# An adapter with weights made per batch: two late matmul groups moved, one batch tiled otherwise, repeated waits dropped

## The chip, the core and the metric

The kernel runs on one core of one Trainium2 chip. The metric is the device time in microseconds (us) of one execution. Three runs of the kernel before took 210.18, 210.27 and 210.38 us; the median is 210.27 us. One further execution was profiled: it took 210.3 us, and its span, from the first to the last instruction, is 208.4 us.

## The reference

Everything is float32. `x` is (4, 1024, 512): B = 4 batches, L = 1024 rows, D = 512 columns. `h` is (4, 128), one vector of H = 128 per batch, and N = 128 is the width of the bottleneck.

```
dWd  = ((h @ Wdd.T + bdd) * 0.1).reshape(B, N, D)     # Wdd is (65536, 128): 33.6 MB
dWu  = ((h @ Wdu.T + bdu) * 0.1).reshape(B, D, N)     # Wdu is (65536, 128): 33.6 MB
down = relu(einsum('bld,bnd->bln', x, Wd + dWd) + bd)
up   = einsum('bln,bdn->bld', down, Wu + dWu) + bu
out  = x + up
```

The two big matrices are each read once; `x` (8.4 MB) is read and `out` (8.4 MB) written.

## The kernel before, in words

**Two phases of loading.** Wdd and then Wdu come in 32 chunks of 1 MB each (lines 236 to 285). All loads of these, the eight 1 MB pieces of `x` and all stores are issued by SP (SyncE), in one order that is written out; an instruction that waits on SP holds everything behind it. VectorE transposes each chunk in 32x32 blocks (L315; the last chunk in two halves, L373). TensorE sums two chunks at a time against `st`, which holds the four `h` vectors (`sum_pair`, L552; `sum_last_pair`, L680), into the PSUM tiles `acc`. Four chunks make a group; ScalarE copies it (`g_rows`, L391) and TensorE turns it (`turn_down_group`, L563 and L566, in phase one; `turn_up_group`, L578, in phase two). The result is `wd_b` in phase one and `wu_b` in phase two: each group g of Wdu brings 64 of the 512 columns of `wu_b`. GpSimd adds these (L516, L519), and VectorE adds the last group (L326, L329).

**The adapter itself runs beside phase two.** The 1024 rows of a batch are 8 blocks of 128 (I = 8). Three kinds of work are interleaved on TensorE after the sums of chunk t, by the tables `TURN_AT`, `DOWN_AT` and `UP_COUNT`:

- `turn_x_unit(j)`: transposes two blocks of `x` (16 in all, j = 0 to 15), in two halves m = 2j and 2j + 1 of four transposes each (L635). ScalarE copies each half to `xt` (L433), and GpSimd adds `bu` to `x` (L500).
- `down_unit(j)`, in short D_j: the down sum of the same two blocks, four matmuls of 256 columns into the PSUM tile `dn` (L646). ScalarE copies it with ReLU to `down` (L441, `down_ready`). There is one `dn`, so D_j waits for the copy of D_(j-1).
- `up_unit(e)`, in short U_e: a number of blocks by a number of columns of the output, 512 elements per partition at most, with `down` as the stationary operand (L670). `UNITS` lists 34 of them as (batch, first block, blocks, first column, columns). A unit of four blocks by 128 columns is called quarter-D here, one of two blocks by 256 columns half-D. A unit waits for `down_ready` of all its blocks. U0 to U20 are copied by ScalarE (L451) and added to `x` in SBUF by GpSimd (L507, `pool_final`); U21 to U33 are added by VectorE straight from PSUM (L358, `dve_final`). Transposes and units share four PSUM banks in a ring (`BANK_USE`).

Every float32 matmul and transpose is recorded as two passes, so D_j has 8, a quarter-D unit 8 and a half-D unit 4 matmul records.

**The tail** begins when the last chunk has been transposed. TensorE then does, in this order: the last pair sum, X14, the last turned group, X15, U19 to U23, D14, U24, U25, D15, U26 to U33. X14 and X15 are the last two transposed pairs of blocks. D14 and D15 make the blocks 4 to 7 of batch 3, which only U30 to U33 use.

**Stores.** `STORES` has 14 of them, in SP's order after all loads: the first column halves of batches 0, 1 and 2 (1 MB each) and of half of batch 3, then the second halves in pieces of 256 or 512 KB, and last blocks 4 and 5 and blocks 6 and 7 of batch 3 over all columns (512 KB each). Each waits for the units inside it; the last one waits for U33.

Of the kernel before, what the change touches and what calls it, by code (L numbers as in the profile page):

```python
# [7 lines left out]
B, L, D, N, H = 4, 1024, 512, 128, 128  # L8
# [29 lines left out]
I = L // P  # L38
# [6 lines left out]
PIECE_OF = [j // 2 for j in range(DOWN_UNITS)]  # L45
# [7 lines left out]
HALF = D // 2  # L53
QD = D // 4
EARLY = 2
UNITS = [(b, i, 4, q * QD, QD) for q in range(2) for b in range(EARLY) for i in range(0, I, 4)]
UNITS += [(b, i, 2, 0, HALF) for b in range(EARLY, B) for i in range(0, I, 2)][:-2]
UNITS += [(b, i, 4, 2 * QD, QD) for b in range(EARLY) for i in range(0, I, 4)]
UNITS += [(2, 0, 4, 2 * QD, QD), (2, 4, 2, 2 * QD, QD), (2, 6, 2, 2 * QD, QD)]
UNITS += [(0, 0, 2, 3 * QD, QD), (0, 2, 2, 3 * QD, QD), (0, 4, 4, 3 * QD, QD)]  # L60
UNITS += [(b, i, 4, 3 * QD, QD) for b in range(1, B - 1) for i in range(0, I, 4)]
UNITS += [(B - 1, i, 2, HALF, HALF) for i in range(0, I - 4, 2)]
UNITS += [(B - 1, i, 2, c, HALF) for i in range(I - 4, I, 2) for c in (0, HALF)]
# [5 lines left out]


TURN_AT = {0: 2, 1: 3, 2: 4, 3: 5, 4: 6, 5: 7, 8: 8, 9: 9, 10: 10, 11: 11, 12: 12, 13: 13}
DOWN_AT = {0: 1, 1: 2, 2: 3, 3: 4, 4: 5, 5: 6, 6: 7, 9: 8, 10: 9, 11: 10, 12: 11, 13: 12, 15: 13}
LAST_DOWNS = (DOWN_UNITS - 2, DOWN_UNITS - 1)
assert list(TURN_AT.values()) == list(range(2, LAST_DOWNS[0]))
assert list(DOWN_AT.values()) == list(range(1, LAST_DOWNS[0]))
UP_COUNT = {8: 1, 9: 1, 14: 2, 16: 1, 17: 1, 18: 2, 19: 1, 20: 2, 21: 1, 22: 1, 23: 1, 24: 1, 25: 1, 26: 1, 27: 1, 28: 1}
UP_AT, UP_BEFORE_LAST = {}, 0
for _t, _n in UP_COUNT.items():
    UP_AT[_t] = list(range(UP_BEFORE_LAST, UP_BEFORE_LAST + _n))
# [1 line left out]


UP_BEFORE_SUM = UP_BEFORE_LAST
UP_BEFORE_DOWNS = (UP_BEFORE_SUM + 5, UP_BEFORE_SUM + 7)
assert UP_BEFORE_SUM < POOL_UNITS <= UP_BEFORE_DOWNS[0]


# [23 lines left out]
def later(count, back):  # L111

    return not isinstance(count, int) or count >= back


def hyper_adapter(nc, x, cond, Wd, bd, Wu, bu, Wdd, bdd, Wdu, bdu, out):
# [10 lines left out]
    with ctx:  # L127
# [6 lines left out]
        def sem(name):  # L134
            return ctx.enter_context(nc.semaphore(name))
# [41 lines left out]
        x_loaded = [sem(f"x_loaded{h}") for h in range(len(X_PIECES))]  # L177
# [18 lines left out]
        g_ready = sem("g_ready")  # L196
# [25 lines left out]
        def bank_of(kind, n):  # L222
            return bank[USE_OF[kind, n] % BANK_RING]
# [5 lines left out]
        def unit_size(e):  # L229
            _, rows, cols = unit_at(e)  # L230
            return (rows.stop - rows.start) * (cols.stop - cols.start)
# [149 lines left out]
        def _(act):  # L381
# [55 lines left out]
            def copy_down(j):  # L437

                act.wait_ge(down_summed, j + 1)
                b, i0 = j // BATCH_UNITS, j % BATCH_UNITS * UNIT_I  # L440
                nc.scalar.activation(down[:, b, i0:i0 + UNIT_I, :],  # L441
                                     dn[:].rearrange("p (i l) -> p i l", i=UNIT_I),
                                     ACT.Relu, bias=bd_col[:]).then_inc(down_ready, 1)
# [10 lines left out]
            def copy_x_unit(j):  # L454
                copy_x(2 * j)
                copy_x(2 * j + 1)
# [7 lines left out]
            for t in range(CHUNKS - PAIR):  # L464
# [5 lines left out]
                if t in TURN_AT:  # L470
                    copy_x_unit(TURN_AT[t])
                if t in DOWN_AT:
                    copy_down(DOWN_AT[t])
                for e in UP_AT.get(t, ()):
# [62 lines left out]
        def _(pe):  # L537
# [8 lines left out]
            def sum_pair(c, low, slot, a):  # L546

                pe.wait_ge(wt_ready, c + PAIR)
                for r in range(R):
                    for h in range(PAIR):  # L550
                        place = 2 * (r % 2) + h
                        last = nc.tensor.matmul(a[TILE * place:TILE * (place + 1)],  # L552
                                                st[:, r, low * TILE:(low + 1) * TILE], wt[:, slot + h, r],
                                                start=low == 0 and r < 2, stop=low == 1 and r >= 2)
                last.then_inc(pair_summed, 1)

            def turn_down_group(g, n):

                pe.wait_ge(g_ready, g + 1)
                if later(g, 1):  # L560
                    pe.wait_ge(group_ready, g)
                for k in range(C):
                    nc.tensor.matmul(gt[:, k, 0:PART], g_rows[:, n, k * P:(k + 1) * P], fold[:],  # L563
                                     start=True, stop=False)
                    pick = ident[:, bass.ds(g * SQ, SQ)].unsqueeze(2).to_broadcast([P, SQ, B])
                    last = nc.tensor.matmul(gt[:, k, 0:PART], base_d[:, k * P:(k + 1) * P], pick,  # L566
                                            start=False, stop=True)
                last.then_inc(g_turned, 1)
# [14 lines left out]
            def turn(it):  # L583
                for u in range(TURN_CHUNKS):
                    c, s, n = TURN_CHUNKS * it + u, u % SLOTS, u // SLOTS
                    if s == 0 and later(it, 1):
                        pe.wait_ge(g_ready, 2 * it + n - 1)
                    if s % PAIR == 0:
                        sum_pair(c, s // PAIR, u % T_RING, acc[n][:])
                    if u == 6 and isinstance(it, int):  # L590

                        pe.wait_ge(base_u_summed, 1)
                        for k in range(C):
                            last = nc.tensor.transpose(bank[1][:, k * P:(k + 1) * P], wu_nat[:, k], ident[:])  # L594
                        last.then_inc(base_turned, 1)
                        pe.wait_ge(bias_loaded, 16 * 2)
                        pe.wait_ge(ones_ready, 1)
                        nc.tensor.matmul(bank[2][:, 0:D], ones, bu_row, start=True, stop=True)  # L598
                        nc.tensor.matmul(bank[3][:, 0:1], bd_row, ones[:, 0:1], start=True, stop=True
                                         ).then_inc(bias_spread, 1)  # L600
                    if u == 1 and not isinstance(it, int):
                        turn_down_group(2 * it - 1, 1)
                    if u == SLOTS + 1:
                        if isinstance(it, int):
                            pe.wait_ge(fold_ready, 1)
                            pe.wait_ge(base_d_summed, 1)
                        turn_down_group(2 * it, 0)

            turn(0)
            with pe.Fori(1, TURNS) as it:  # L610
                turn(it)
# [17 lines left out]
            def turn_x(m):  # L629
                j, c0 = m // 2, m % 2 * BANK_C  # L630
                b, i0 = j // BATCH_UNITS, j % BATCH_UNITS * UNIT_I
                pe.wait_ge(x_loaded[PIECE_OF[j]], 16)
                wait_bank("x", m)
                for n, (c, i) in enumerate((c, i) for c in range(c0, c0 + BANK_C) for i in range(UNIT_I)):
                    last = nc.tensor.transpose(bank_of("x", m)[:, n * P:(n + 1) * P],  # L635
                                               xs[:, b, i0 + i, c * P:(c + 1) * P], ident[:])
                last.then_inc(x_turned, 1)
# [12 lines left out]
            def turn_x_unit(j):  # L650
                turn_x(2 * j)
                turn_x(2 * j + 1)
# [36 lines left out]
            down_unit(0)  # L689
            for t in range(CHUNKS - PAIR):  # L690
                c, s, g = CHUNKS + t, t % SLOTS, (CHUNKS + t) // SLOTS
                if s == 0:
                    pe.wait_ge(g_ready, g - 1)
                if s % PAIR == 0:
                    sum_pair(c, s // PAIR, t % T_RING_U, acc[g % 2][:])
                if s == SLOTS - 1:
                    turn_up_group(g)
                if t in TURN_AT:
                    turn_x_unit(TURN_AT[t])
                if t in DOWN_AT:  # L700
                    down_unit(DOWN_AT[t])
                for e in UP_AT.get(t, ()):
                    up_unit(e)
# [7 lines left out]
            turn_x_unit(LAST_DOWNS[1])  # L711
            for e in range(UP_BEFORE_SUM, UP_BEFORE_DOWNS[0]):
                up_unit(e)
            down_unit(LAST_DOWNS[0])
            for e in range(UP_BEFORE_DOWNS[0], UP_BEFORE_DOWNS[1]):
                up_unit(e)
            down_unit(LAST_DOWNS[1])
            for e in range(UP_BEFORE_DOWNS[1], UP_UNITS):
                up_unit(e)
# [26 lines left out]
```

## Time and profile before

| | |
|---|---|
| median of three runs | 210.27 us |
| the profiled execution, its span | 210.3 us, 208.4 us |
| HBM read, written | 76.55 MB, 8.39 MB |
| TensorE matmul, VectorE busy | 171.6 us (82%), 160.1 us (77%) |
| ScalarE, GpSimd busy | 57.3 us (28%), 74.1 us (36%) |
| mean granted TensorE clock | 0.946 |
| last chunk's transposes begin | 183.83 us |
| VectorE's last addition begins | 204.65 us |

Part 2 of the profile's page cuts the span into 40 slices of 5.2 us. A line of the chain of waits gives a start, a duration and what ran or was awaited. A line of the timeline gives a start, a duration, the engine (PE is TensorE's matmuls, PEld its weight loads, ACT ScalarE, POOL GpSimd, SPq a DMA issued by SyncE), the line of the kernel, the operation, the tiles, and in brackets the idle time before it and what ended that. The ends of matmuls are modelled by the profiler.

### The profile page before, as it was taken

The page shows a single profiled execution, that of the slowest core. Times are in us where ns is not written, and L with a number is a line of the kernel's source. Part 1 is how long each engine was busy: PE and PEld are TensorE (multiplying, and loading weights), DVE is VectorE, ACT ScalarE, POOL GpSimd, SP SyncE. Part 2 cuts the span into 40 slices and gives each one's busy share as a digit, 9 for nine tenths or more (in the row PEclk, how much of TensorE's full clock was granted, in tenths as well). Part 3 has the DMA queues.
Part 4 walks back from the last instruction along what each step waited for, and adds up shares of the span by engine and source line. Part 5 has one row for each costly group of instructions (what it writes and reads, how often), then busy time and mean ns, then how long its engine had stood idle before and what let it go on. Part 6 is the DMA issues. An engine that isn't in the chain of part 4 may idle for free.

```text
span 208.4 us, 3089 instructions
## 1 busy us (share of the span) xinstructions
PE 171.6 (82%) x1164; PEld 103.0 (49%) x1164; DVE 160.1 (77%) x89; ACT 57.3 (28%) x104; POOL 74.1 (36%) x59
## 2 busy tenths in 40 slices
PE   1066599847776993899999989999999988889992
PEld 0011173423321740376866748668656544549991
DVE  2868998899999999944854976468998999974373
ACT  2000014101111112043554535545425442416100
POOL 2000000000000000026857927988467977558300
PEclk9999999997975599699999999999999999999998
DMA  5999999999999999999999999999999999999998
GB/s 219 422 415 423 421 421 417 421 426 421 417 426 423 421 417 425 423 426 420 415 423 425 420 412 425 417 425 421 420 420 420 421 420 417 426 389 386 371 348 312
DMA packets 18617, 85.11 MB, mean 408 GB/s; under 512 B 1447, under 2 KB 8620, under 8 KB 9389
## 3 DMA queue, kind: packets, MB, share of 16 engines
q1 hardware_dynamic: 18592, 84.94, 99.8%
q8 instruction: 8, 0.13, 0.3%
q14 instruction: 5, 0.03, 0.0%
q10 hardware_dynamic: 12, 0.00, 0.0%
HBM read 76.55 MB, written 8.39 MB: 408 GB/s over the span
## 4 chain that ended last, share of the span: by engine, by line
DMA 64%; DVE 18%; PE 15%; issue 1%; SPq 0%; DVEq 0%
DMA w<-in_L_cond_Wdu_dram 38%; DMA w<-in_L_cond_Wdd_dram 26%; DVE wt L315 17%; PE bank L670 5%; PE acc L552 4%; PE dn L646 2%; DVE wt L373 1%; PE gt L563 1%; PE bank L635 1%; PE gt L566 1%; PE acc L680 1%; PE bank L598 1%; SPq L242 0%; DVE xs L358 0%; PE bank L594 0%
## 5 line engine op out<-in xcount | busy, mean ns | idle before, releaser
L315 DVE STREAM_TRANSPOSE wt<-w 128x2048 f32<-128x2048 f32 x63 | 145.5, 2311 | 31.9 <-DMA w<-in_L_cond_Wdu_dram 22.8
L552 PE MATMUL acc<-wt,st 128*32 128x512 f32 x496 | 72.6, 712 | 28.6 <-DVE wt L315 28.6
L500 POOL TENSOR_TENSOR xs<-xs,bu_all 128x1024 f32<-128x1024 f32 x16 | 37.8, 2368 | 102.7 <-PE bank L635 102.7
L552 PEld LDWEIGHTS acc<-wt,st 128*32 128x32 f32 x496 | 14.9, 122 | 67.8 <-issue 35.4
L670 PE MATMUL bank<-wu_b,down 128*128 128x128 f32 (+1 forms) x208 | 31.7, 303 | 0.0
L670 PEld LDWEIGHTS bank<-wu_b,down 128*128 128x128 f32 x208 | 27.7, 191 | 7.8 <-issue 5.0
L646 PE MATMUL dn<-xt,wd_b 128*128 128x256 f32 x128 | 30.5, 381 | 0.0
L507 POOL TENSOR_TENSOR xs<-up_s,xs 128x512 f32<-128x512 f32 (+1 forms) x21 | 25.4, 1226 | 12.1 <-ACT up_s L451 12.1
L646 PEld LDWEIGHTS dn<-xt,wd_b 128*128 128x128 f32 x128 | 23.1, 190 | 3.5 <-issue 0.8
L391 ACT ACTIVATE g_rows<-acc 128x512 f32<-128x512 f32 x16 | 9.6, 598 | 45.8 <-PE acc L552 43.4
L433 ACT ACTIVATE xt<-bank 128x512 f32<-128x512 f32 x32 | 17.4, 596 | 8.8 <-PE bank L635 8.8
L635 PEld LDWEIGHTS bank<-ident,xs 128*128 128x128 f32 x128 | 14.2, 141 | 6.6 <-issue 6.3
L398 ACT ACTIVATE wd_b<-gt 128x256 f32 (+1 forms) x8 | 5.0, 628 | 43.8 <-PE gt L566 43.8
L635 PE MATMUL bank<-ident,xs 128*128 128x128 f32 x128 | 17.0, 276 | 0.0
L451 ACT ACTIVATE up_s<-bank 128x512 f32<-128x512 f32 (+1 forms) x21 | 12.1, 577 | 16.0 <-PE bank L670 15.8
L563 PEld LDWEIGHTS gt<-fold,g_rows 128*128 128x128 f32 x64 | 11.5, 225 | 8.1 <-issue 7.2
L563 PE MATMUL gt<-fold,g_rows 128*128 128x64 f32 x64 | 14.7, 316 | 0.0
L566 PE MATMUL gt<-ident,base_d 128*128 (+1 forms) x64 | 14.4, 312 | 0.0
L358 DVE TENSOR_TENSOR xs<-bank,xs 128x512 f32<-128x512 f32 (+1 forms) x13 | 8.5, 651 | 6.8 <-PE bank L670 6.7
L441 ACT ACTIVATE down<-dn,bd_col 128x256 f32<-128x256 f32 x16 | 7.6, 474 | 21.6 <-PE dn L646 21.6
L566 PEld LDWEIGHTS gt<-ident,base_d 128*128 128x128 f32 x64 | 11.7, 227 | 0.0
L516 POOL TENSOR_TENSOR base_d<-base_d 128x256 f32<-128x256 f32 x7 | 5.1, 735 | 4.3 <-ACT base_d L425 4.3
(35 smaller groups left out, 36.3 us busy)
## 6 DMA issues: line engine op xcount, KB each, us to landing
w<-in_L_cond_Wdd_dram SPq DMA_DIRECT2D x32, 1024.0 KB, 7.4
w<-in_L_cond_Wdu_dram SPq DMA_DIRECT2D x32, 1024.0 KB, 10.0
xs<-in_x_dram SPq DMA_DIRECT2D x8, 1024.0 KB, 12.2
out_dram<-xs SPq DMA_DIRECT2D x9, 512.0 KB, 3.6
out_dram<-xs SPq DMA_DIRECT2D x3, 1024.0 KB, 12.1
out_dram<-xs SPq DMA_DIRECT2D x2, 256.0 KB, 4.5
base_d<-in_L_cond_Wd_dram SPq DMA_DIRECT2D x1, 256.0 KB, 7.2
down<-in_L_cond_bdd_dram SPq DMA_DIRECT2D x1, 256.0 KB, 7.3
```

The lines of the kernel that those rows point to most:

```text
L315: nc.vector.transpose(wt[:, tslot].rearrange("p r (k j) -> p k r j", j=QUAD), w[:, slot, :].rearrange("p (k r h) -> p k r h", r=R, h=QUAD) ...
L391: nc.scalar.activation(g_rows[:, n].rearrange("p (j k) -> p j k", k=K), acc[n][:].rearrange("p (k j) -> p j k", k=K), ACT.Copy, scale=DELT ...
L433: nc.scalar.activation(xt[:, j % XT_RING, c0:c0 + BANK_C, :], bank_of("x", m)[:].rearrange("p (c l) -> p c l", c=BANK_C), ACT.Copy).then_i ...
L451: nc.scalar.activation(up_s[:, e % UP_RING, 0:size], bank_of("up", e)[:, 0:size], ACT.Copy).then_inc(up_copied, 1)
L500: nc.gpsimd.tensor_tensor(xs[:, b, i0:i0 + UNIT_I], xs[:, b, i0:i0 + UNIT_I], bu_pair, ALU.add).then_inc(bu_added, 1)
L507: nc.gpsimd.tensor_tensor(unit_x(e), unit_sums(e, up_s[:, e % UP_RING]), unit_x(e), ALU.add).then_inc(pool_final, 1)
L552: last = nc.tensor.matmul(a[TILE * place:TILE * (place + 1)], st[:, r, low * TILE:(low + 1) * TILE], wt[:, slot + h, r], start=low == 0 an ...
L563: nc.tensor.matmul(gt[:, k, 0:PART], g_rows[:, n, k * P:(k + 1) * P], fold[:], start=True, stop=False)
L566: last = nc.tensor.matmul(gt[:, k, 0:PART], base_d[:, k * P:(k + 1) * P], pick, start=False, stop=True)
L635: last = nc.tensor.transpose(bank_of("x", m)[:, n * P:(n + 1) * P], xs[:, b, i0 + i, c * P:(c + 1) * P], ident[:])
L646: last = nc.tensor.matmul(dn[:], wd_b[:, c, j // BATCH_UNITS], xt[:, j % XT_RING, c], start=c == 0, stop=c == C - 1)
L670: last = nc.tensor.matmul(place[:, n], down[:, b, i], wu_b[:, b, cols], start=True, stop=True)
```

## The change

Three edits. D14 and D15 stand directly in front of U30 and U32, the first units that read them. Batch 1's first column half is no longer four quarter-D units but four half-D units, later in the list, and the tables of what follows which chunk are fitted to that (D13 after chunk 14 instead of 15; two units after chunks 24 and 26 and none after 14). TensorE no longer waits for `g_ready` ahead of the first pair sum of a group, and waits for a piece of `x` once instead of ahead of each half transposed unit.

```
-UNITS = [(b, i, 4, q * QD, QD) for q in range(2) for b in range(EARLY) for i in range(0, I, 4)]
-UNITS += [(b, i, 2, 0, HALF) for b in range(EARLY, B) for i in range(0, I, 2)][:-2]
+UNITS = [(0, i, 4, q * QD, QD) for q in range(2) for i in range(0, I, 4)]
+UNITS += [(b, i, 2, 0, HALF) for b in range(1, B) for i in range(0, I, 2)][:-2]
...
-DOWN_AT = {0: 1, 1: 2, 2: 3, 3: 4, 4: 5, 5: 6, 6: 7, 9: 8, 10: 9, 11: 10, 12: 11, 13: 12, 15: 13}
+DOWN_AT = {0: 1, 1: 2, 2: 3, 3: 4, 4: 5, 5: 6, 6: 7, 9: 8, 10: 9, 11: 10, 12: 11, 13: 12, 14: 13}
...
-UP_COUNT = {8: 1, 9: 1, 14: 2, 16: 1, 17: 1, 18: 2, 19: 1, 20: 2, 21: 1, 22: 1, 23: 1, 24: 1, 25: 1, 26: 1, 27: 1, 28: 1}
+UP_COUNT = {8: 1, 9: 1, 16: 1, 17: 1, 18: 2, 19: 1, 20: 2, 21: 1, 22: 1, 23: 1, 24: 2, 25: 1, 26: 2, 27: 1, 28: 1}
...
-UP_BEFORE_DOWNS = (UP_BEFORE_SUM + 5, UP_BEFORE_SUM + 7)
+UP_BEFORE_DOWNS = (UP_BEFORE_SUM + 11, UP_BEFORE_SUM + 13)
...
                     c, s, n = TURN_CHUNKS * it + u, u % SLOTS, u // SLOTS
-                    if s == 0 and later(it, 1):
-                        pe.wait_ge(g_ready, 2 * it + n - 1)
...
                 b, i0 = j // BATCH_UNITS, j % BATCH_UNITS * UNIT_I
-                pe.wait_ge(x_loaded[PIECE_OF[j]], 16)
+                if m % 2 == 0 and (j == 0 or PIECE_OF[j] != PIECE_OF[j - 1]):
+                    pe.wait_ge(x_loaded[PIECE_OF[j]], 16)
...
                 c, s, g = CHUNKS + t, t % SLOTS, (CHUNKS + t) // SLOTS
-                if s == 0:
-                    pe.wait_ge(g_ready, g - 1)
```

With it the tail of TensorE reads: last pair sum, X14, the last turned group, X15, U19 to U29, D14, U30, U31, D15, U32, U33. The number of units (34), their sizes from U19 on, and the stores are as before.

## Rows read from the trace of the kernel before

**Rows 1.** The page's part 2: granted clock and GB/s in 40 slices.
```profile
PEclk9999999997975599699999999999999999999998
GB/s 219 422 415 423 421 421 417 421 426 421 417 426 423 421 417 425 423 426 420 415 423 425 420 412 425 417 425 421 420 420 420 421 420 417 426 389 386 371 348 312
```

**Rows 2.** The chain of waits, from the last chunk's transfer on: start, us, what.
```profile
176.25 7.56 DMA w<-in_L_cond_Wdu_dram
...
186.25 1.07 PE acc L680 x16
187.32 1.02 PE bank L635 x8
...
188.78 0.87 PE bank L635 x8
189.66 2.68 PE bank L670 x24
192.34 1.73 PE dn L646 x8
194.07 1.78 PE bank L670 x16
195.85 1.73 PE dn L646 x8
197.58 6.98 PE bank L670 x40
```

**Rows 3.** The timeline: VectorE's last addition, U33.
```profile
204.65 0.69 DVE L358 TENSOR_TENSOR xs<-bank,xs 128x512 f32<-128x512 f32 x1 [0.17 <-PE bank L670]
```

**Rows 4.** The timeline and the tile view: the last store's issue, its time to landing.
```profile
205.37 0.34 SPq L267 DMA_DIRECT2D out_dram<-xs  x1
DMA to landing us min/median/max: 2.6/2.6/2.6
```

**Rows 5.** The timeline: D15, its copy, the unit behind it.
```profile
195.69 1.89 PE L646 MATMUL dn<-xt,wd_b 128*128 128x256 f32 x8
197.42 7.13 PE L670 MATMUL bank<-wu_b,down 128*128 128x128 f32 x40
197.62 0.47 ACT L441 ACTIVATE down<-dn,bd_col 128x256 f32<-128x256 f32 x1 [3.04 <-PE dn L646]
```

**Rows 6.** The timeline: a half-D unit's weight loads, its copy, GpSimd behind it.
```profile
168.18 0.73 PEld L670 LDWEIGHTS bank<-wu_b,down 128*128 128x128 f32 x4 [0.84 <-issue]
169.35 0.60 ACT L451 ACTIVATE up_s<-bank 128x512 f32<-128x512 f32 x1 [0.43 <-PE bank L670]
170.09 1.27 POOL L507 TENSOR_TENSOR xs<-up_s,xs 128x512 f32<-128x512 f32 x1 [1.08 <-ACT up_s L451]
```

**Rows 7.** The timeline: an idle TensorE released by VectorE.
```profile
3.03 0.41 DVE L297 COPY xt<-xt 4x512 f32<-4x512 f32 x1 [3.03 <-DMA xt<-in_cond_dram]
3.50 0.50 PEld L542 LDWEIGHTS gt<-ident,xt 4*128 4x128 f32 x4 [3.50 <-DVE xt L297]
```

**Rows 8.** Windows: engines' busy time, then granted clock, DMA share and GB/s.
```profile
184.00:196.00 12.00, 11.16 (x106) 9.50 (x105) 5.74 (x9) 4.43 (x9) 7.40 (x6) 1.00 1.08 385
...
199.75:200.25 0.50, 0.50 (x4) 0.45 (x3) 0.41 (x1) 0.00 (x0) 0.00 (x0) 1.00 0.64 225
200.25:204.50 4.25, 4.25 (x20) 3.43 (x19) 3.46 (x5) 0.00 (x0) 0.00 (x0) 1.00 1.04 352
...
206.00:206.25 0.25, 0.00 (x0) 0.00 (x0) 0.00 (x0) 0.00 (x0) 0.00 (x0) 1.00 0.59 213
206.25:207.50 1.25, 0.00 (x0) 0.00 (x0) 0.00 (x0) 0.00 (x0) 0.00 (x0) 0.64 1.00 406
```

**Rows 9.** The timeline: TensorE's pair sums for chunk 28 and for the last pair.
```profile
181.33 1.92 PE L552 MATMUL acc<-wt,st 128*32 128x512 f32 x16 [0.71 <-DVE wt L315]
185.13 2.19 PE L680 MATMUL acc<-wt,st 128*32 128x256 f32 x32 [0.79 <-DVE wt L373]
```

**Rows 10.** The timeline: the first pair sum, at the lower clock.
```profile
10.67 3.64 PE L552 MATMUL acc<-wt,st 128*32 128x512 f32 x16 [6.58 <-DVE wt L315]
```

## The prediction, made before the changed kernel was run

> **What bounds the kernel now.** I read the 40 slices first, then the chain of waits, then the tail in the timeline and in windows. From the second slice to the 35th the transfers run at 412 to 426 GB/s [rows 1]: loading is bound by bandwidth, and nothing that TensorE does beside it shows in the time unless it delays a load. The last chunk's transfer ends at 183.8 us (176.25 + 7.56) [rows 2]. Whatever the change brings must therefore show in the last 24.6 us of the span.
>
> Two things run there side by side: 8.39 MB of stores, and a block of TensorE work that has to end before the last store can be issued. The chain of waits says which of them ends last. From 186.25 to 204.56 us it is TensorE alone, piece after piece without a hole: pair sum, X14, the turned group, X15, 24 passes of units (2.68 us), D14 (1.73), 16 passes (1.78), D15 (1.73), 40 passes (6.98) [rows 2]. Then VectorE adds U33 from 204.65 for 0.69 us [rows 3], and the last store is issued at 205.37, 0.03 us behind that addition's end. It lands 2.6 us later, at 207.97, and the span ends at 208.43, another 0.46 us later [rows 4]. So the end is TensorE's last pass + 0.09 + 0.69 + 0.03 + 2.6 + 0.46 us.
>
> The other candidate, the DMA queue, is full at 385 GB/s only until 196 us. After that it has holes: 225 GB/s around 200, 352 up to 204.5, and 213 (share 0.59) just ahead of the last store's packets [rows 8]. The stores go out as VectorE finishes units, and the queue waits for them. Between 206.25 and 207.5 us 406 GB/s x 1.25 us = 0.51 MB moved, which is the last store of 512 KB and nothing else; its packets start some 0.88 us after its issue, behind a hole. It did not stand in a queue.
>
> **The change part by part.** *D14 and D15 moved.* No pass is added or removed: 16 passes of 0.217 us (1.73 / 8) stand elsewhere. What changes is what lies between each D and the unit that reads it. A unit that reads D14's blocks needs ScalarE's copy of them. Before, U24 and U25 (1.78 us) lay behind D14, and then D15; behind D15 lay four units. ScalarE's copies ran beside these and cost nothing. After the change U30 stands directly behind D14 and U32 directly behind D15, U30's and U32's wait for `down_ready` is at the head of TensorE's queue, and everything behind it (U31, D15; U33) waits with it. TensorE has nothing to do in the meantime.
>
> The stall, counted from the first pass of a D at time s. Without a wait the next unit's first pass starts at s + 1.73 (195.69 and 197.42). With it: ScalarE's copy starts at s + 1.93 (197.62) and takes 0.47 us, so it ends at s + 2.40 [rows 5]. To this comes the handover to TensorE's weight load. The trace before has no row in which an idle TensorE is released by ScalarE. The nearest is VectorE's release, 3.50 - (3.03 + 0.41) = 0.06 us [rows 7]; ScalarE to GpSimd takes 0.14 (169.95 to 170.09) [rows 6]. I take 0.06. Then comes the first weight load, which a stream of passes hides and a pause lays bare. Its price by a half-D unit behind a pause: ScalarE starts 1.17 us after the unit's first weight load (168.18 to 169.35) [rows 6]; the passes take 3 x 0.217 us to the start of the last, which by D15's record lasts 1.89 - 7 x 0.217 = 0.37, 1.02 in all, and ScalarE starts 0.04 behind a last pass's modelled end (195.69 + 1.89 to 197.62) [rows 5]. What is left is 1.17 - 1.02 - 0.04 = 0.11 us. The stall is 2.40 + 0.06 + 0.11 - 1.73 = 0.84 us, and two of them 1.7 us.
>
> Bounds of a stall: 0.68 if the weight load hides wholly or the handover is free, and 1.08 with 0.14 us of handover and the slow start of the first eight passes behind a break, 1.02 against 0.87 us [rows 2]. Two give 1.35 to 2.15 us.
>
> What the move gives: U24 and U25 end 1.73 us earlier and U26 to U29 3.46 us earlier, so the stores of the second column halves go out up to 3.5 us earlier and fill the holes around 200 us. But the last store still waits for U33, which is behind all of TensorE's work. What comes early there only makes the queue idle longer ahead of the end: U33 would be added by 205.34 + 1.7 = 207.0 us, and U31 before it by 1.73 (U32 and U33) + 0.84 + 1.73 (D15), by 202.7 us. I count the gain as nothing.
>
> *Batch 1's first half in half-D units.* Four units of 8 x 0.111 = 0.89 us (1.78 / 2) become four of 4 x 0.217 = 0.87 us [rows 2]: 0.1 us of TensorE in all, in the stage bound by the loads, so nothing. What moves are 8 passes each from chunk 14 to chunks 18 to 26. Chunk 26 gets one unit more, 0.87 us, ahead of the sums for chunk 28, where TensorE had 0.71 us of idle time; the 0.16 us that are left over go into the 0.79 us ahead of the last pair's sums, which wait for VectorE and thereby for the last load [rows 9]. If that cover were gone too, 0.87 us would go onto the path once. The stores of the first column halves need U3, U7, U11 and U13; U13 is now behind chunk 24, two pair sums ahead of the row at 181.33, while the DMA engines are busy to 196 us with what is queued. D13 moves one chunk earlier behind D12, whose copy of 0.47 us is waited for where TensorE has room. I take 0 for all of this.
>
> *Repeated waits dropped.* In phase one and in phase two up to 183.8 us they stand under the loads: nothing. In the tail three are left, ahead of the second half of X14 and both halves of X15. Every one was long fulfilled, and the passes there go at 0.87 / 8 = 0.109 us, like a stream without waits; the most that they could give is the 0.15 us by which X14 is slower than X15 (1.02 against 0.87) [rows 2], which I put down to the break ahead of it. I take 0, bounds -0.15 to 0.
>
> *The sum.* The profiled execution's 210.3 us + 1.7 = 212.0 us; it stands 0.03 us above the median of 210.27 us, so the same figure is the forecast for the median. With the bounds: 211.5 to 212.5.
>
> One rule speaks for less. The last store now meets DMA engines that have been idle for some time, where before the previous store's packets ended only about 0.1 us ahead of it [rows 8]. Between its last packets (207.5) and its landing (207.97) the row leaves 0.47 us [rows 4, 8]. The Trainium skill, "DMA: Bandwidth & Descriptors", section "Latency and other measured facts", says that access to HBM takes 0.2 us on average and 2 us under high load, and that a lighter load makes the fixed cost of a DMA smaller. By the rows the landing stays at 2.6 us and the sum at 212.0; by the rule part of the 0.47 us would go, which is the second rival.
>
> **The rivals.** *The stores set the end (faster).* Place: the last 12 us of the DMA queue. If the last store's packets had to stand behind those of the stores before it, what counts is bytes over rate, and earlier units are worth their time. Price: the holes against 385 GB/s are 5.2 us x (14 + 37) GB/s = 0.27 MB in slices 38 and 39 (371 and 348 GB/s, up to 203.2 us) [rows 1], 0.04 MB up to 204.5 and 0.04 MB at 206 [rows 8], 0.35 MB or 0.9 us: 209.4 us. For it: the DMA engines are at a share over 1.0 for most of the tail. Against it: SyncE issues the last store 0.03 us behind VectorE, and its packets come behind a hole. It decides from the point where the store ahead ends later than some 0.85 us behind the last issue; here it ends before that, and after the change earlier still.
>
> *The last store lands sooner.* By up to 0.47 us: 211.5 us.
>
> *Nothing moves.* If TensorE's queue could have the weights of U30 and U32 in time, or the stalls came with an equal gain at the waits that are dropped, the time would be 210.3. Against it: `down` is the stationary operand, so the very first weight load must wait for the copy, and the waits dropped in the tail show no gap.
>
> *The clock falls.* It is at 1.00 from 184 us on and falls only after TensorE has ended [rows 8]. Earlier it was at its lower level (1.2 of 2.4 GHz) in parts of slices 10 to 17 [rows 1], and the first pair sum took 3.64 us at that level against 1.92 [rows 9, 10]. If the two pauses brought it down for U32 and U33, these would take another 1.73 us: 213.7. Against it: pauses of 0.7 to 0.8 us at 181 and 185 us left the clock alone (nine tenths and over in the last slices but one) [rows 1, 9].
>
> **How the numbers follow.** What a measurement of this kernel can tell from no change is about 0.2%, 0.42 us. Forecast 212.0 us, own range 211.5 to 212.5: 0.79. Last store sooner, 211.5: 0.07. Stores set the end, 209.4: 0.05. Nothing moves, 210.3: 0.05. Clock falls, 213.7: 0.04. The first two and the last are slower: 0.90; faster 0.05; same 0.05. The range reaches down to 211.0, for a stall at its lower bound together with a sooner landing (210.3 + 1.35 - 0.47 = 211.2, and 0.15 from the waits), and up to 212.6.
>
> **What would show it.** In the profile after: D14's eight passes at about 197.6 us and D15's at about 201.9, each followed by ScalarE's copy and a gap of 0.8 us on TensorE that `down` L441 ends, with these copies on the chain of waits; VectorE's last addition at about 206.35; the store of U24 and those behind it 1.7 to 3.5 us earlier, a DMA share far under 1 for some 2 us ahead of 207.9, and a landing 2.6 us behind the last issue. The load phase should end at 183.8 as before. It is wrong if TensorE shows no gap behind a D, if its last pass ends by 204.6 us, or if the last store's packets follow the ones before without a hole; then the queue was the bound. If the pair sums of the last chunk start later than 186.25, the moved units were not covered.

## The result, and the profile after

The changed kernel takes 212.16 us (median of six runs, 212.02 to 212.9); the kernel before took 210.28 us in the runs beside it. The ratio is 1.0091, with a 95% interval of 1.0073 to 1.0108: slower by 1.9 us. The forecast was 212.0 us, with a range of 211.0 to 212.6. Three single executions among the runs below, of 896.94, 221.74 and 255.85 us, are left out of the ranges and ratios.

The chain of waits of the changed kernel, from the last chunk's transposes on (start, us, what), answers to [rows 2]:

```profile
184.21 2.38 DVE wt L373 x2
...
186.64 1.07 PE acc L679 x16
...
190.04 7.98 PE bank L669 x64
198.02 1.74 PE dn L645 x8
199.76 0.02 issue
199.79 0.48 ACT down L441
200.27 0.04 issue
200.31 1.99 PE bank L669 x8
202.31 1.74 PE dn L645 x8
204.05 0.02 issue
204.07 0.48 ACT down L441
204.56 0.04 issue
204.60 2.01 PE bank L669 x8
```

Before, this stretch was TensorE alone. Now ScalarE's copy of `dn` stands in it twice, and each group of 8 passes behind a copy takes 1.99 to 2.01 us in place of 1.73. Of these 0.26 us about 0.10 are a longer record (1.99 against the 1.89 of [rows 5]): the first pass and its weight load start at the same moment, 200.31. The other 0.16 us is the overlap with the work ahead, which a pause takes away: in a stream the next record starts 0.16 us before the last one's modelled end (195.69 + 1.89 - 197.42). From D14's first pass to the end of U31 it is 202.31 - 198.02 = 4.29 us; the same 16 passes take 2 x 1.73 = 3.46 in a stream. That is a stall of 0.83 us, and behind D15 it is 206.61 - 202.31 - 3.46 = 0.84: together 1.67 us.

The timeline of the changed kernel shows the same from the side of the engines (in brackets the idle time before, and its releaser):

```profile
199.79 0.47 ACT L441 ACTIVATE down<-dn,bd_col 128x256 f32<-128x256 f32 x1 [8.43 <-PE dn L645]
200.31 1.59 PEld L669 LDWEIGHTS bank<-wu_b,down 128*128 128x128 f32 x8 [0.97 <-ACT down L441]
200.31 1.99 PE L669 MATMUL bank<-wu_b,down 128*128 128x256 f32 x8 [0.56 <-ACT down L441]
...
206.70 0.69 DVE L358 TENSOR_TENSOR xs<-bank,xs 128x512 f32<-128x512 f32 x1 [0.17 <-PE bank L669]
```

VectorE's last addition begins at 206.70, 2.05 us later than in [rows 3]. 1.67 us of it are the stalls; 0.38 us came earlier, since the last chunk's transposes begin at 184.21 and not at 183.83. The prediction named a last pair sum later than 186.25 as the sign that the moved units are not covered, and it starts at 186.64. But it follows the transposes by 2.43 us, against 2.42 before, so TensorE did not delay it; VectorE already stands 0.5 us later at 144 us (144.44 against 143.95), after a wait of 3.12 us for a load at 131 us, where it waited 2.71 before. The profiled execution took 212.35 us, also 2.05 above the one of before.

The windows of the changed kernel (busy time by engine, granted clock, DMA share, GB/s) answer to [rows 8], and SyncE's last store with its landing to [rows 4]:

```profile
204.00:206.00 2.00, 1.44 (x8) 1.25 (x8) 0.16 (x1) 0.47 (x1) 0.00 (x0) 1.00 0.97 368
...
206.00:207.90 1.90, 0.59 (x3) 0.19 (x1) 1.22 (x2) 0.00 (x0) 0.00 (x0) 1.00 0.05 19
...
208.30:209.50 1.20, 0.00 (x0) 0.00 (x0) 0.00 (x0) 0.00 (x0) 0.00 (x0) 1.00 0.99 406
```

```profile
207.42 0.34 SPq L267 DMA_DIRECT2D out_dram<-xs  x1
DMA to landing us min/median/max: 2.6/2.6/2.6
```

The stores that were ready early have left the DMA engines with next to nothing for 1.9 us (a share of 0.05), and then the last store takes its 2.6 us all the same. The granted clock stayed at 1.00 through U32 and U33.

### The profile page after: what moved, and what is told of

Same layout as the page of the kernel before. It is cut to its first block, busy times and chain, and to the rows that moved or that the text cites. A ratio compares the mean times of both kernels' runs of the same rounds, so it can differ in the third digit from the quotient of the medians.

```text
span 210.5 us, 3027 instructions
## 1 busy us (share of the span) xinstructions
PE 171.0 (81%) x1148; PEld 101.9 (48%) x1148; DVE 160.1 (76%) x89; ACT 57.3 (27%) x104; POOL 74.2 (35%) x59
## 4 chain that ended last, share of the span: by engine, by line
DMA 67%; DVE 19%; PE 9%; issue 2%; ACT 0%; SPq 0%; DVEq 0%
DMA w<-in_L_cond_Wdu_dram 37%; DMA w<-in_L_cond_Wdd_dram 30%; DVE wt L315 18%; PE bank L669 6%; PE dn L645 2%; DVE wt L373 1%; PE bank L634 1%; PE acc L679 1%; ACT down L441 0%; SPq L242 0%; DVE xs L358 0%; PE gt L578 0%; DVE down L347 0%; DVEq L357 0%
## 5 line engine op out<-in xcount | busy, mean ns | idle before, releaser
L552 PE MATMUL acc<-wt,st 128*32 128x512 f32 x496 | 71.4, 703 | 31.0 <-DVE wt L315 30.6
L552 PEld LDWEIGHTS acc<-wt,st 128*32 128x32 f32 x496 | 14.4, 121 | 70.1 <-DVE wt L315 38.3
L669 PEld LDWEIGHTS bank<-wu_b,down 128*128 128x128 f32 x192 | 26.4, 191 | 9.1 <-issue 5.0
```

What stands on the lines that cost most here:

```text
L669: last = nc.tensor.matmul(place[:, n], down[:, b, i], wu_b[:, b, cols], start=True, stop=True)
```

## The experiments

Times are medians; beside each stands the ratio to the kernel before, run on the same chip, with its 95% interval. The medians of the kernel before beside them are 210.25 us (late down sums, one unit between, tiling and waits together), 210.41 us (waits or tiling alone, padded, the attempt to be faster) and 210.26 us (the rest); a ratio is not exactly the quotient of two medians.

**Only the two down sums late.**

```
-UP_BEFORE_DOWNS = (UP_BEFORE_SUM + 5, UP_BEFORE_SUM + 7)
+UP_BEFORE_DOWNS = (UP_BEFORE_SUM + 11, UP_BEFORE_SUM + 13)
```

> The kernel before with one edit of three: D14 and D15 directly in front of U30 and U32. If the two stalls behind them are the whole of the loss: 210.3 + 1.7 = 212.0 us (211.7 to 212.3), two gaps of 0.8 us on TensorE that ScalarE's copy L441 ends. If the other two edits carry a part of it (the last chunk's transposes begin 0.4 us later in the changed kernel's trace): 211.5 to 211.8 us. If the stores set the end: below 210.3 us.

Measured: 212.17 us, 1.0089 (1.0074 to 1.0104). This edit alone is slower by as much as the whole change. The last chunk's transposes begin at 183.71 us here, so the 0.38 us of the profile after don't belong to this edit.

**One of them late.** `(UP_BEFORE_SUM + 5, UP_BEFORE_SUM + 13)`: D14 stays in front of U24.

> The kernel before with D14 left in front of U24 and D15 alone put directly in front of U32: one stall instead of two. Stalls as the cause: 210.3 + 0.85 = 211.15 us. A cost that does not go by the number of stalls (the order of the stores, the clock): 212.0 or 210.3 us.

Measured: 211.09 us, 1.0047 (1.0031 to 1.0062), half the loss. TensorE waits once for ScalarE in this kernel's tail, 0.6 us by the view of waits, where the changed kernel has two such waits (us in total, times, longest):

```profile
PE bank L670 <- ACT down L441: 0.6, 1, 0.6
```

**Late, but with one unit between.** `(UP_BEFORE_SUM + 10, UP_BEFORE_SUM + 12)` in the kernel before.

> The kernel before with D14 in front of U29 and D15 in front of U31: nearly as late as in the change, but with one half-D unit of 0.87 us between each down sum and the first unit that reads it. Stalls of 0.84 us as the cause, and TensorE as the bound: covered, 210.3 us (210.2 to 210.5), although U24 to U28 and their stores come 1.7 to 3.5 us earlier. If the stores set the end: 209.4 us. If a late position costs by itself: 211 us or more.

Measured: 210.12 us, 0.9996 (0.9985 to 1.0006). The timeline of its TensorE has D14 (196.47) and D15 (199.93) with no idle time behind them:

```profile
196.47 1.89 PE L646 MATMUL dn<-xt,wd_b 128*128 128x256 f32 x8
198.20 1.89 PE L670 MATMUL bank<-wu_b,down 128*128 128x256 f32 x8
199.93 1.89 PE L646 MATMUL dn<-xt,wd_b 128*128 128x256 f32 x8
201.65 2.75 PE L670 MATMUL bank<-wu_b,down 128*128 128x256 f32 x12
```

One half-D unit of 0.87 us covers a stall of 0.84. The units ahead of D14 come earlier here too, and the time doesn't move: the stores don't set the end.

**The other two edits alone.** The changed kernel with `(UP_BEFORE_SUM + 5, UP_BEFORE_SUM + 7)`.

> The changed kernel with D14 and D15 put back where they were before (in front of U24 and U26), so the new tiling of batch 1 and the dropped waits alone. If these are hidden under the loads: 210.3 us (210.1 to 210.5), the last chunk's transposes at 183.8 us. If they delay the loads or the last sums: 210.5 to 210.7 us. If dropped waits give TensorE time in the tail: 210.1 us.

Measured: 211.55 us with a spread of 210.12 to 213.06; 1.0049 (1.0021 to 1.0076). I had counted these edits at nothing, and alone they are slower by 0.4 to 1.6 us. In the profiled run TensorE and VectorE are on time (last chunk's transposes 183.70, VectorE's last addition 204.53, even 0.12 us earlier than before). What is late is the landing of the last store, 4.1 us in place of 2.6, and the whole execution of 211.51 us is 1.2 us above the profiled one of before. Its windows:

```profile
205.00:206.00 1.00, 0.00 (x0) 0.00 (x0) 0.22 (x1) 0.00 (x0) 0.00 (x0) 1.00 0.98 392
206.00:207.00 1.00, 0.00 (x0) 0.00 (x0) 0.00 (x0) 0.00 (x0) 0.00 (x0) 1.00 0.73 293
207.00:208.00 1.00, 0.00 (x0) 0.00 (x0) 0.00 (x0) 0.00 (x0) 0.00 (x0) 1.00 0.63 254
208.00:209.00 1.00, 0.00 (x0) 0.00 (x0) 0.00 (x0) 0.00 (x0) 0.00 (x0) 0.65 0.05 20
```

The last row is what to look for: a share of 0.05 over a microsecond is about one DMA engine of 16 (0.0625) at work while 15 are done. The DMA view of 207.8 to 208.9 us says the same, seven packets (number, MB, share of 16 engines), 0.063 x 16 = one engine:

```profile
q1 hardware_dynamic: 7, 0.03, 6.3%
```

The kernel before has 0.00 from 208 us on:

```profile
208.00:209.00 1.00, 0.00 (x0) 0.00 (x0) 0.00 (x0) 0.00 (x0) 0.00 (x0) 0.50 0.00 0
```

The DMA view of 203.5 to 205 us names a candidate for what held it up, a load of instructions (packets, MB, share). That it went to the same engine is not in the trace:

```profile
q8 instruction: 1, 0.02, 3.9%
```

0.039 x 16 engines x 1.5 us = 0.94 us of one engine. In the kernel before such a load stands between 196 and 197 us, with the holes of the queue behind it [rows 8]. The Trainium skill, "Runtime: NRT & Kernel Launch", section "Instruction fetch mechanics", says that an engine's instructions come in blocks of 16 KiB, 256 instructions; the profile's page of the kernel before agrees (8 such loads, 0.13 MB). So a shorter program can move the moment of each load.

**The waits dropped alone, and the tiling alone**, each in the kernel before.

> The kernel before with the repeated waits dropped and nothing else. First theory (the time of a load of instructions): TensorE's program is 34 instructions shorter than before (2365 against 2399), so the last 16 KB load of instructions, at 196.5 us in the kernel before and at 203.8 us in the run with tiling and waits, falls in between, at about 200 us; it holds up one DMA engine's store packets by 1 us, which the holes behind it cover in part: 210.3 to 211.0 us, with a wider spread than before. Rival (the dropped waits themselves are good or bad on TensorE): no shift of that load, and 210.1 or 211.5 us by TensorE's last pass.

Measured: 211.25 us, 210.28 to 212.82; 1.0035 (1.0012 to 1.0059).

> The kernel before with batch 1 in half-D units and the tables fitted to it, the waits as before. First theory: 30 instructions fewer (2369 against 2399), the load of instructions at about 200 us, 210.3 to 211.0 us. Rival (the tiling costs by itself, through the units after chunks 24 and 26): 211.5 us with the last pair sum later than 186.3 us.

Measured: 210.62 us, 210.13 to 212.84, with seven of twelve runs under 210.9; 1.0030 (1.0004 to 1.0057). Both are slower by a little and spread wider, as forecast (the dropped waits by more than the 211.0 us forecast at most), but the step behind it failed: the last loads of instructions did not move to about 200 us. They stand at about 190 us in the one profile (none later) and at about 188 us in the other (the next after the stores). In both the last store lands in 2.6 us. The first one's profile is late in the loads instead: its last chunk's transposes begin 0.9 us later than before.

```profile
184.72 2.38 DVE wt L373 x2
```

The second one's profile shows nothing late, but it took 210.26 us and is one of the seven quick runs. So these two show that either edit costs alone, and not where.

**The same program length as before.** The kernel with tiling and waits, and in phase two, ahead of the transposes of each of 26 chunks, five fulfilled waits on TensorE:

```
+                if t < 26:
+                    for _ in range(5):
+                        pe.wait_ge(st_ready, Q)
```

> The kernel of the run with tiling and waits (211.55 us, 210.12 to 213.06), with 130 fulfilled waits added to TensorE's program in phase two, under the loads, which bring it from 2335 to 2396 instructions (before: 2399). First theory: the last load of instructions is back at about 196.5 us, every store lands in about 2.6 us behind its last issue, 210.2 us and a spread under 1 us. Rival (tiling and waits cost by what they do on the engines): 211.5 us as without the padding, or more by the added waits.

Measured: 210.23 us, 209.94 to 210.71; 0.9983 (0.9966 to 1.0000). The last load of instructions is back between 192 and 199 us, and the last store lands in 2.6 us. Waits that do nothing, added to the program, took 1.3 us off: what tiling and dropped waits cost goes away without touching the work on the engines.

**A held-up DMA engine by itself.** The kernel before, and on ScalarE behind `dve_final` 9:

```
+            act.wait_ge(dve_final, 9)
+            for n in range(3):
+                act.dma_start(w[0:1, n, :], wdd_chunks[n][0:1]).then_inc(spare_loaded, 16)
+            act.wait_ge(spare_loaded, 48)
```

> The kernel before, and in addition three loads of 8 KB in one piece each, which nobody reads, issued by ScalarE when VectorE has added U29 (about 202 us). They stand for a load of 16 KB of instructions late in the tail: about 0.9 us of work on one of the 16 DMA engines. If one held-up DMA engine sets the landing of the last stores: 210.8 to 211.6 us, the last store lands 3.2 us or more behind its issue. If a load of 24 KB is lost in 8.4 MB of stores: 210.3 us.

Measured: 211.21 us, 1.0050 (1.0037 to 1.0063), for 24 KB beside 8.4 MB of stores. The last store lands in 3.5 us, and the window behind it has again one DMA engine alone:

```profile
208.00:209.00 1.00, 0.00 (x0) 0.00 (x0) 0.00 (x0) 0.00 (x0) 0.00 (x0) 0.50 0.03 12
```

The same with `dve_final` 1, ahead of the late down copies:

> The same three loads, issued at about 191.5 us, behind VectorE's U21. The holes of the DMA queue behind them (0.7 us in all up to 204 us) let the engine catch up: 210.3 to 210.6 us. If every such load costs its own time wherever it stands: as much as the late ones, 210.8 to 211.6 us.

Measured: 210.24 us, 0.9997 (0.9974 to 1.0020), the last store lands in 2.7 us. The same loads cost 0.95 us when they are issued at 201.88 us, and nothing that can be told from no change when they are issued at 191.81 us.

**The changed kernel with the padding.**

> The changed kernel with the 130 fulfilled waits of the padded run in TensorE's program (2396 instructions in place of 2335). The two stalls of 0.84 us as the whole of the loss: 212.0 us (211.7 to 212.2). If the shorter program carried a part of it: 210.6 to 211.6 us.

Measured: 211.87 us (211.83 to 211.99), 1.0076 (1.0063 to 1.0089): 1.6 us over the kernel before, which the two stalls account for.

**The changed kernel, padded, with one unit between.** `(UP_BEFORE_SUM + 10, UP_BEFORE_SUM + 12)`.

> The changed kernel, padded as above, with one half-D unit between each late down sum and its first reader (D14 in front of U29, D15 in front of U31). Stalls as the cause of the loss: 210.1 us (209.9 to 210.4), level with the kernel before, no gap on TensorE behind a down sum. If the early stores are worth something once no stall stands behind them: under 209.9 us.

Measured: 210.14 us, 0.9992 (0.9984 to 1.0001). All three edits together are level with the kernel before once the stalls are covered; the early stores bring nothing that can be told from no change.

**An attempt to be faster.** The kernel with one unit between, and

```
-UP_COUNT = {..., 27: 1, 28: 1}
+UP_COUNT = {..., 27: 1, 28: 1, 29: 2}
```

which puts U19 and U20 ahead of the last pair sum (`UP_BEFORE_SUM` grows by 2 with it, so one unit between is written + 8 and + 10).

> A kernel meant to be faster: the kernel before with one unit between each late down sum and its first reader, and besides U19 and U20 (8 passes, 0.89 us) ahead of the last pair sum, where TensorE has 0.8 us of idle time. TensorE as the bound: its last pass 0.9 us earlier, 210.1 - 0.9 = 209.2 us, or 209.4 us where the stores become the bound. If the moved units delay the last pair sum: 210.1 us.

Measured: 210.81 us, 209.99 to 212.98; 0.9998 (0.9979 to 1.0018). It fell short by its best run too. The timeline of its TensorE says why:

```profile
190.26 1.04 PE L635 MATMUL bank<-ident,xs 128*128 128x128 f32 x8
191.87 6.46 PE L670 MATMUL bank<-wu_b,down 128*128 128x128 f32 x52 [0.57 <-issue]
```

U19 and U20 stood behind X15, where they covered VectorE's two additions of the last group; with them gone U21 has to wait for `last_added`, as the kernel's code has it: the second addition ends at 191.77 us and U21's passes start at 191.87. (The view puts the 0.57 us down to "issue".) From the last chunk's transposes (185.47) to VectorE's last addition (206.21) it is 20.74 us, against 20.82 before (183.83 to 204.65) [rows 3]: of 0.89 us moved, 0.08 were gained. The profiled execution is the slowest of the twelve, 212.98 us: its last transposes begin 1.64 us late, and its last store lands only in 3.8 us, with no load of instructions behind 200 us. Neither is explained.

## Why the prediction was right

The step that carries the forecast, two bare round trips through ScalarE on the path that ends last, is what the runs show.

**The bound.** TensorE's chain and the last store set the end, not the rate of the stores: with the early units and no stall the time stays (210.12 and 210.14 us), and each stall comes through in full (0.84 us for one, 1.6 for two, at 211.09 and 211.87).

**The size of a stall.** Worked out at 0.84 us from ScalarE's 0.47, two handovers and a weight load; the profile after has 0.83 and 0.84. The handover from ScalarE to TensorE that no row of before showed is 200.31 - 200.27 = 0.04 to 0.05 us, where 0.06 was taken, and the bare weight load is 0.10 us where 0.11 was taken. A slip in the bounds changed nothing: 0.68 us is what is left of a stall without both terms (0.84 - 0.06 - 0.11 = 0.67), not without either one, which gives 0.73 or 0.78. D14's passes stand at 197.9 and D15's at 202.1, 197.6 and 201.9 in the forecast, which is the 0.38 us of late loads less 0.1.

**The gain counted as nothing.** The early stores only lengthened the idle time ahead of the last one.

**The rival of the faster landing** falls: 2.6 us behind an idle queue as behind a busy one. The rule of the Trainium skill beside it ("DMA: Bandwidth & Descriptors", section "Latency and other measured facts"), that a lighter load makes a DMA's fixed cost smaller, is not seen, to the 0.1 us of the view. It was hardly tested, since behind the last store's packets nothing else moves in either kernel. **The stores as the bound, no movement, and a fallen clock** fall by the windows and the ratio. One reading behind the clock's price was wrong: the view grants 1.00, not the lower clock, around the pair sum of [rows 10]. The price stands by another pair sum of the kernel before, which takes the same 3.64 us from 64.23 on, where the windows grant 0.50:

```profile
64.23 3.64 PE L552 MATMUL acc<-wt,st 128*32 128x512 f32 x16 [1.82 <-DVE wt L315]
64.00:66.00 2.00, 1.77 (x12) 0.46 (x16) 1.73 (x2) 0.00 (x0) 0.00 (x0) 0.50 0.98 410
```

**What was wrong without changing the sign.** "Edits 2 and 3 cost nothing" was right of the engines and wrong of the time when they stand alone: 0.2 to 1.3 us in the median. For the two together a late landing behind one held-up DMA engine is shown in the profile, and the padding takes the cost away; that the load of the program's instructions is what holds it up is argued from its moment and from the three small loads that do the same. For either one alone the place stays open. My sum did not have this term, and that it does not spoil the forecast is in part luck: the early stores and the stalls leave idle time ahead of the last store, in which a held-up engine can catch up. The late edit alone shows it. Its profile has a load of instructions between 202 and 203 us, nearly as late as in the kernel with tiling and waits. Then its queue is nearly idle from 205.5 to 207.7 us, and its last store lands in 2.6 us all the same (DMA view of 202 to 203 us, windows, tile view):

```profile
q8 instruction: 1, 0.02, 5.8%
...
205.50:207.70 2.20, 0.59 (x3) 0.19 (x1) 1.22 (x2) 0.00 (x0) 0.00 (x0) 1.00 0.08 34
...
DMA to landing us min/median/max: 2.6/2.6/2.6
```

The changed kernel's own profile has no such load between 190 and 210.4 us, so there was nothing to catch up with in it. 212.16 us unpadded against 211.87 padded leaves 0.3 us; the two were not run side by side, and the late edit alone, with the length of before, also took 212.17, so that 0.3 us stays open. So does the 0.38 us in the loads of the profile after: with the same edits the padded run's last transposes begin at 183.80 us.

## What to carry to other kernels

A producer directly in front of its reader, with a copy on another engine between them, costs the whole round trip (0.83 and 0.84 us here); put as much work between them as that trip is long (here one unit of 0.87 us for 0.84), and ask of each unit that you move away what it was covering. Work that comes early is worth nothing to a chain whose last link hasn't moved. After an edit that should be hidden, look at the window behind the last store: a DMA share of one sixteenth there points to one held-up DMA engine, not to work that takes longer.

## What the runs showed of the hardware that was not expected

A DMA lands with the slowest of its 16 engines: 4.1 us in place of 2.6 with one engine left at work. A load of 16 KB of instructions takes one of them for about 0.94 us (worked out above from its share), and three loads of 8 KB that stand for it cost 0.95 us when issued at 201.88 us and nothing to be told from noise at 191.81.

The moment of such a load moves with the program, but not by its length alone. The last one ahead of the end stands at 196 us in the kernel before, at 203 with tiling and waits, at 197 with these padded, at 189 and 188 with either one alone, at 189 in the changed kernel, and at 202 with only the down sums moved, which does the same passes in another order. In medians and spreads: 64 instructions fewer on TensorE (2335 against 2399, as counted with the expectations) gave 211.55 us with a spread of 2.9 us, and 61 instructions more, from 130 waits without a purpose, gave 210.23 with one of 0.8. The changed kernel is as short as the first of these and spreads over 0.9 us.
